# Mamba-2 layer with an FFN: the product between chunks taken out of the decay matrices, and four decay units a tile in place of six

## What is computed

```python
A_dt = (dt * A)                                    # per token and head, negative
A_cum = jnp.cumsum(A_dt, axis=-1)                  # within a chunk
L = jnp.exp(_segsum(A_dt))                         # exp(A_cum[l] - A_cum[s]) for s <= l
Y_diag = jnp.einsum('bzlhn,bzshn,bhzls,bzshp->bzlhp', Cc, Bc, L, xch)
decay_states = jnp.exp(A_cum[..., -1:] - A_cum)
states = jnp.einsum('bzlhn,bhzl,bzlhp->bzhpn', Bc, decay_states, xch)
...                                                # prev: the state ahead of a chunk
Y_off = jnp.einsum('bzlhn,bzhpn,bhzl->bzlhp', Cc, prev, jnp.exp(A_cum))
Y = (Y_diag + Y_off).reshape(b, s, H, P) + hs * D[None, None, :, None]
g = y * jax.nn.silu(gate)                          # then normed by group, times out_proj
```

## Time and profile before

| what | us |
|---|---|
| median of 3 runs | 1920.87 |
| lowest and highest | 1920.41, 1922.65 |
| the profiled execution | 1922.98 |
| its span in the profile | 1921.2 |

### The profile page before, as it was taken

One profiled execution on the slowest core, in us unless ns is written; L12 is line 12 of the kernel. 1 busy time (PEld: TensorE's weight loads), 2 busy tenths in 40 slices (PEclk: granted clock), 3 DMA queues, 4 the chain that ended last, 5 costly groups with the idle time before them and its releaser, 6 DMA issues.

```text
span 1921.2 us, 37314 instructions
## 1 busy us (share of the span) xinstructions
PE 1818.6 (95%) x11192; PEld 1482.3 (77%) x11192; DVE 1310.7 (68%) x2149; ACT 918.2 (48%) x1660; POOL 1014.9 (53%) x802
## 2 busy tenths in 40 slices
PE   4799999999999999999999999999999977989898
PEld 3577787778777877787778777877787756878887
DVE  6788738873887388638863886388638848777776
ACT  2566526653665366536653664366436632212221
POOL 6266636663666366636663666366536665333220
PEclk9899999999999999999999999999999988999999
DMA  2211101110111011101110111011101110111101
GB/s 90 60 52 49 37 12 51 51 33 12 51 51 33 12 51 51 33 12 51 51 33 12 51 51 33 12 51 51 33 12 52 40 41 22 45 44 34 42 11 45
DMA packets 43568, 74.83 MB, mean 39 GB/s; under 512 B 10321, under 2 KB 11473, under 8 KB 43537
## 3 DMA queue, kind: packets, MB, share of 16 engines
q1 hardware_dynamic: 43536, 74.43, 12.3%
HBM read 70.35 MB, written 4.06 MB: 39 GB/s over the span
## 4 chain that ended last, share of the span: by engine, by line
PE 87%; DVE 8%; issue 2%; ACT 1%; POOL 1%; DMA 0%; SPq 0%; DVEq 0%; POOLq 0%; ACTq 0%
PE proj L738 15%; PE proj L740 15%; PE proj L739 15%; PE y L870 6%; PE y L924 5%; PE y L926 5%; PE y L925 5%; PE y L860 3%; PE trb L837 3%; PE diff L846 3%; DVE gated L1229 2%; PE misc L846 1%; PE y L738 1%; PE y L739 1%; PE y L740 1%
## 5 line engine op out<-in xcount | busy, mean ns | idle before, releaser
L738 PE MATMUL proj<-xhi,w_hi 128*128 128x512 f32 x1088 | 464.8, 427 | 0.6 <-DVE v L1052 0.6
L740 PE MATMUL proj<-xhi,w_lo 128*128 128x512 f32 x1088 | 425.3, 391 | 0.0
L739 PE MATMUL proj<-xlo,w_hi 128*128 128x512 f32 x1088 | 424.7, 390 | 0.0
L391 POOL TENSOR_TENSOR w_lo<-w_raw,w_hi 128x512 fp32r<-128x512 f32 x144 | 183.6, 1294 | 223.6 <-ACT w_hi L516 223.6
L1052 DVE SCALAR_TENSOR_TENSOR v<-proj,par_sb,v 128x510 f32<-128x510 f32 (+2 forms) x384 | 281.8, 742 | 23.3 <-ACT v L538 19.9
L447 POOL TENSOR_TENSOR g_lo<-gated,g_hi 128x512 fp32r<-128x512 f32 x128 | 164.7, 1290 | 190.1 <-ACT g_hi L670 189.4
L738 PEld LDWEIGHTS proj<-xhi,w_hi 128*128 128x128 f32 x1088 | 204.5, 188 | 70.1 <-DVE v L1052 7.2
L740 PEld LDWEIGHTS proj<-xhi,w_lo 128*128 128x128 f32 x1088 | 204.2, 188 | 46.1
L739 PEld LDWEIGHTS proj<-xlo,w_hi 128*128 128x128 f32 x1088 | 204.8, 188 | 38.5
L1147 DVE TENSOR_TENSOR M<-diff,cb 128x512 f32<-128x512 f32 x256 | 170.3, 686 | 81.3 <-ACT diff L625 81.3
L924 PE MATMUL y<-wo_hi,g_hi 128*128 128x512 f32 x512 | 204.1, 399 | 5.5 <-POOL g_lo L447 5.1
(11 more groups left out here) (179 smaller groups left out, 3733.4 us busy)
## 6 DMA issues: line engine op xcount, KB each, us to landing
w_raw<-in_win SPq DMA_DIRECT2D x144, 256.0 KB, 2.7
wo_raw<-in_wout SPq DMA_DIRECT2D x64, 256.0 KB, 2.5
M<-in_w SPq DMA_DIRECT2D x14, 512.0 KB, 3.3
cb<-in_w SPq DMA_DIRECT2D x7, 512.0 KB, 3.3
row_l<-rows_l SPq DMA_DIRECT2D x192, 6.0 KB
resid<-in_x SPq DMA_DIRECT2D x8, 256.0 KB, 6.6
out<-resid SPq DMA_DIRECT2D x8, 256.0 KB, 2.0
rows_l<-gated SPq DMA_DIRECT2D x9, 128.0 KB, 2.5
```

The lines of the kernel that those rows point to most:

```text
L391: e.tensor_tensor(w_lo[:, slot, i, :], w_raw[:, i, :], w_hi[:, slot, i, :].bitcast(F32), ALU.subtract).then_inc(split.sem, 1)
L738: e.matmul(o, hi_l, hi_r, start=first, stop=False)
L739: e.matmul(o, hi_l, lo_r, start=False, stop=False)
L740: return e.matmul(o, lo_l, hi_r, start=False, stop=last)
```

## The change

The exponents of kind 1 (from chunk 0 to chunk 1) are gone, and with them two decay matrices a tile. Their part of y is made another way. The input of chunk 0 is weighted once with dt * exp(sum of what follows in the chunk) (`dt_rest`, made at the start; `xrest`, two VectorE operations of 256 columns a tile). One fp32 product per sequence, with C.B from chunk 0 to chunk 1 (`cb[:, 1]`) moving and xrest of both heads as the weights, goes to the bank misc (`y_past`). VectorE multiplies it with exp of the running sums of chunk 1 (`decayed`, loaded from DRAM and spread over the 64 partitions of a head; `scale_past`), and adds it to the second chunk of y, after the two sums (`late`). `y_own` holds the other 16 narrow products. The four decay units use two banks. Units 1 and 2 of the projection stand around exponents 2 and 3 now.

row_l is loaded from the same DRAM rows as row_r; the sign is in the rows of ones. Both are single, not doubled, so SyncE loads the next tile's rows when all four exponents of this tile are made. Behind scale_past it loads decayed, in two DMAs. GpSimd's gated waits for the last add in both halves. At the start, the reversed sums and the negated copies are gone.

```diff
-        row_r = sb("row_r", [P, 2, 2, TOK], BF16)
-        row_l = sb("row_l", [P, 2, 2, 3 * P], BF16)
+        row_r = sb("row_r", [P, 2, TOK], BF16)
+        row_l = sb("row_l", [P, 2, 2 * P], BF16)
+        dt_rest = sb("dt_rest", [P, B, H])
+        xrest = sb("xrest", [P, B, P])
+        decayed = sb("decayed", [P, HALF])
...
 # SyncE
             def step(g, j, par_, nxt, nxt2):
...
                 if nxt:
-                    sp.wait_ge(dready.sem, dready.at(g, j, 1))
-                    load_rows(TPG * g + j + 1, 1 - par_)
+                    sp.wait_ge(dready.sem, dready.at(g, j, UNITS))
+                    load_rows(TPG * g + j + 1)
                 if nxt2:
                     load_pair(9 * g + j + 3, split.at(g, j, 0))
+                if nxt:
+                    sp.wait_ge(scaled.sem, scaled.at(g, j, 1))
+                    load_decayed(TPG * g + j + 1)
...
 # GpSimd
                 for h in range(2):
-                    pool.wait_ge(ysum.sem, ysum.at(g, j, h + 1))
+                    pool.wait_ge(ysum.sem, ysum.at(g, j, 3))
...
 # ScalarE, step
                 decays(0)
...
                     tap3(0, w, ready.at(g, j, 1), silu.at(g, j, -1))
-                decay(2)
-                decay(3)
                 if nxt:
                     tap3(1, w, ready.at(g, j, 2), silu.at(g, j, 0))
                     act.wait_ge(gdone.sem, gdone.at(g, j, 0))
                     hs_tanh(hs[:, 1 - par_, :], 0, taken.at(g, j, 1))
+                decays(2)
                 if nxt2:
                     act.wait_ge(ready.sem, ready.at(g, j, 0))
                     upper_pair(par_, 9 * g + j + 3)
-                decays(4)
                 if nxt:
                     hs_tanh(hs[:, 1 - par_, :], 1, taken.at(g, j, 2))
...
 # TensorE, step
+                def y_past():
                     pe.wait_ge(xdts.sem, xdts.at(g, j, 2))
                     pe.wait_ge(ysum.sem, ysum.at(g, j, 0))
+                    for b in range(B):
+                        mm = e.matmul(misc[:, b * P:(b + 1) * P], xrest[:, b, :], cb[:, 1, b * P:(b + 1) * P],
+                                      start=True, stop=True)
+                    mm.then_inc(yready.sem, 1)
+
+                def y_own():
+                    pe.wait_ge(mdone.sem, mdone.at(g, j, UNITS))
...
                 turn(1)
+                if nxt:
+                    unit(1)
                 exponents(2)
                 exponents(3)
                 if nxt:
-                    unit(1)
-                y_first()
-                exponents(4)
-                exponents(5)
-                if nxt:
                     unit(2)
+                y_past()
+                if nxt:
                     unit(3)
-                y_second()
+                y_own()
...
 # VectorE, step
+                    early = trb[:, :].rearrange("p (b z a f) -> p z b a f", b=2, z=2, a=2)[:, 0, :, :, :]
+                    rest = dt_rest[:, 2 * h:2 * h + 2, bass.ds(2 * t, 2)].unsqueeze(3).broadcast_to([P, 2, 2, HD])
+                    e.tensor_tensor(xrest[:, 2 * h:2 * h + 2, :].rearrange("p b (a f) -> p b a f", a=2), early, rest,
+                                    ALU.mult)
...
+                def scale_past():
+                    dve.wait_ge(yready.sem, yready.at(g, j, 1))
+                    dve.wait_ge(s_grown, (TPG * 32) * g + 32 * j + 32)
+                    e.tensor_tensor(misc[:, :], misc[:, :], decayed[:, :], ALU.mult).then_inc(scaled.sem, 1)
...
                 if nxt:
-                    conv_rest(0, w, tap.at(g, j, 1), convs.at(g, j, 0),
-                              (lambda: weigh(2), lambda: weigh(3)))
+                    conv_rest(0, w, tap.at(g, j, 1), convs.at(g, j, 0))
                     conv_rest(1, w, tap.at(g, j, 2), convs.at(g, j, 2),
                               (lambda: hs_silu(hs[:, 1 - par_, :], 0, tanh.at(g, j, 1)),))
...
-                weigh(4)
-                weigh(5)
+                weigh(2)
+                weigh(3)
                 if nxt:
                     hs_silu(hs[:, 1 - par_, :], 1, tanh.at(g, j, 2))
                     gate_silu(gate[:, 1 - par_, :], 0, tanh.at(g, j, 3))
+                scale_past()
+                if nxt:
                     gate_silu(gate[:, 1 - par_, :], 1, tanh.at(g, j, 4))
...
+                dve.wait_ge(scaled.sem, scaled.at(g, j, 1))
+                dve.wait_ge(ysum.sem, ysum.at(g, j, 2))
+                late = y.rearrange("p (b z l) -> p z b l", b=B, z=2)[:, 1, :, :]
+                e.tensor_tensor(late, late, misc[:, :].rearrange("p (b l) -> p b l", b=B), ALU.add).then_inc(ysum.sem, 1)
```

More of the change, by code:

```diff
@@ L29 @@
 EPS = 1e-5
-UNITS = 6
-SLOT = [0, 1, 2, 3, 0, 1]
+UNITS = 4
 class Tally:
@@ L399, in _ @@
             split_pair(1, 2)
[L401 to L408, removed]
+            pool.wait_ge(s_part[0], 1)
+            e.tensor_tensor(rem, acum, r_part[:, 0, :], ALU.subtract).then_inc(s_rest, 1)
+            pool.wait_ge(s_rest, 1)
+            pool.wait_ge(s_part[1], 1)
+            e.tensor_tensor(r_part[:, 2, :], rem, r_part[:, 1, :], ALU.subtract).then_inc(s_part[2], 1)
             split_pair(1, 4)
@@ L807, in _ @@
             mm.then_inc(s_cum, 1)
-            for b in range(B):
-                mm = e.matmul(misc[:, b * P:(b + 1) * P], dta[:, 2 * b * P:(2 * b + 1) * P],
-                              after, start=True, stop=True)
-            mm.then_inc(s_cum, 1)
+            e.matmul(misc[:, :].rearrange("p (b h) -> p b h", b=B), after,
+                     dta.rearrange("p (b z h) -> p z b h", b=B, z=2)[:, 0, :, :], start=True, stop=True).then_inc(s_cum, 1)
             for n in range(CUM_AFTER + 1, 8):
@@ L850, in unit @@
+                    pe.wait_ge(mdone.sem, mdone.at(g, j, q - 1))
+                    at_l = row_r[:, head, :].rearrange("p (b z l) -> p z b l", b=B, z=2)[:, z, :, :]
+                    e.matmul(diff[q % 2][:, :].rearrange("p (b l) -> p b l", b=B),
+                             row_l[:, head, z * P:(z + 1) * P], at_l, start=True, stop=True).then_inc(dready.sem, 1)
                 def unit(n):
                     project(1 - par_, n // 2, n % 2, split.at(g, j, n // 2 - 1), taken.at(g, j, n - 1))
-                def y_first():
-                    pe.wait_ge(mdone.sem, mdone.at(g, j, 2))
+                def y_past():
@@ L858, in y_first @@
                     for b in range(B):
-                        for head in range(2):
-                            mm = e.matmul(ybank[b // 2][head * HD:(head + 1) * HD, (b % 2) * S:(b % 2) * S + P],
-                                          xdt[:, 2 * b, head * HD:(head + 1) * HD],
-                                          M[:, SLOT[head], b * P:(b + 1) * P], start=True, stop=True)
-                    mm.then_inc(yready.sem, 1)
-                def y_second():
-                    pe.wait_ge(mdone.sem, mdone.at(g, j, 6))
-                    for b in range(B):
-                        for part in range(2):
-                            for head in range(2):
-                                mm = e.matmul(
-                                    ybank[b // 2][head * HD:(head + 1) * HD, (b % 2) * S + P:(b % 2 + 1) * S],
-                                    xdt[:, 2 * b + part, head * HD:(head + 1) * HD],
-                                    M[:, SLOT[2 + 2 * part + head], b * P:(b + 1) * P],
-                                    start=(part == 0), stop=(part == 1))
+                        for z in range(2):
+                            for head in range(2):
+                                first = (b % 2) * S + z * P
+                                mm = e.matmul(ybank[b // 2][head * HD:(head + 1) * HD, first:first + P],
+                                              xdt[:, 2 * b + z, head * HD:(head + 1) * HD],
+                                              M[:, 2 * z + head, b * P:(b + 1) * P], start=True, stop=True)
```

110 lines of the change are left out of this document (48 added, 62 removed).

## The result

| | median us | runs | ratio to the kernel before, 95% interval |
|---|---|---|---|
| before, on the same chip | 1920.64 | 1920.28 to 1922.65 | |
| changed | 1937.92 | 1936.37 to 1942.58 | 1.009, 1.0078 to 1.0102 |

The change costs 17.3 us. The forecast was 1926 with 1916 to 1934 for its own case, and 1906 to 1944 in all: the sign is right and the wide range holds, the size is not right. The rival "Late weights decide" had 1943.

What follows compares the result with a forecast made beforehand. TensorE was taken to bound the kernel, 95% busy. Steps of 16.47 against 16.38 gave +5.7 us, the start -1.6, the last step +1: +5.1 on 1922.98, so 1928.1, a median of 1926, range 1906 to 1944.

Steps and rivals of the forecast that it cites:

- its own case: The forecast's likeliest case for the whole kernel: steps of 16.31 to 16.60, 1916 to 1934 us, chance 0.52.
- Late weights decide: Rival: late w_raw and hs_silu 1's wait for GpSimd delay VectorE; step 16.74, +23 us, 1943 us, chance 0.20.
- What TensorE does less: TensorE's step: two exponent products and y_first go, y_past comes; 0.63 us saved, 15.75 without any wait.
- The wait for the taps: TensorE ahead of unit 2 waits 0.62 us for VectorE's three taps of half 0, making the step 16.37.
- the 35 to 50 that were named: Sign: TensorE idle once a step ahead of unit 2, about 35 to 50 us in total.
- the rival with links of 0.67: Rival: taps follow each other like independent operations, weights cost nothing; steps 16.02 to 16.25, 1898 to 1912 us, chance 0.22.
- Up to here it costs nothing: Late weights on VectorE: free 2.0 into the next step, weighings end at 4.2, second transposes arrive at 4.43; no cost.
- the collision term: hs_silu 1 meets GpSimd's split, 0.3 us; with 0.15 for the last add's wait and branch, 0.1 a step.
- The lateness ahead of it: SyncE's w_raw loads behind the late row loads: w_raw there at 12.35 into the step, cast at 9.24 before.
- The range: Whole-kernel median of 1906 to 1944 us, leaving out the full gain and parts of two rivals.
- The start: Kernel start: two bc silus meet half as much GpSimd work, 3.23 becomes about 1.6, so -1.6 us.

Runs made afterwards that it cites:

- e4: Changed kernel with the w_raw loads ahead of the row loads and y_past ahead of unit 2: 1878.38 us, 0.9767 of before.
- e1: Changed kernel with the two w_raw loads ahead of the row loads in SyncE's queue: 1914.64 us, 0.9962 of before.
- e7: Changed kernel, GpSimd's split waiting for hs_silu 1 and its sums of squares for the next step's hs_silu 0: 1952.82 us, 1.0154 of before.
- e2: Changed kernel with GpSimd's split of w_raw waiting for hs_silu 1 of its step: 1920.7 us, 0.9991 of before.
- e8: Kernel before with row and w_raw loads issued late and ScalarE's w_raw casts behind the last two exponents: 1922.26 us, 1.0009 of before.
- e10: Changed kernel without the last add of each tile: 1917.31 us, 0.9978 of before.
- e9: Changed kernel with w_raw loads first, y_past ahead of unit 2 and GpSimd's start preparation done twice: 1888.57 us, 0.9828 of before.
- e6: Changed kernel with GpSimd's start preparation done a second time on scratch: 1939.8 us, 1.0086 of before.
- e3: Changed kernel with y_past ahead of unit 2 in TensorE's step, weights still late: 1924.45 us, 1.0015 of before.

## Why the prediction was half right

- **What TensorE does less** held. The step without waits was forecast at 15.75; e4, which has next to none, shows 15.85. y_past was a little cheaper than its 0.96: the next unit starts 0.81 behind it (368.68 to 369.49 in e4).
- **The wait for the taps** held to a tenth: unit 2 at 7.93 into a short step against 7.92, 34.5 us in 64 waits, just under the 35 to 50 that were named. The short steps are 16.40 against 16.37. e4 against e1 prices it: 16.45 - 15.88 = 0.57. The three taps of half 0 take 2.51 together (each 0.74 long, the last two starting 0.88 and 0.89 behind the ones ahead, where 0.91 and 0.78 were counted), so the rival with links of 0.67 is out. The Trainium skill, "VectorE: DVE Perf Modes", section "The DRAIN you can't avoid", says that a semaphore between chained Vector operations costs nothing extra. For these taps, which read what the one ahead wrote, the trace does not agree: 0.88 against 0.67 for two independent operations. The row of the taps:

```profile
396.43 2.51 DVE L1037 SCALAR_TENSOR_TENSOR v<-proj,par_sb,v 128x510 f32<-128x510 f32 x3
```

- **"Up to here it costs nothing"** is the step that failed. It had VectorE free 2.0 into the next step, 4.2 after the weighings, with 0.23 of slack to 4.43. e7, where nothing collides, has xrest at 2.75 and the second xrest at 4.88. The missing 0.75 are three small sizes: the tanh of gate 1 at 15.28, not 15.1; from its start to gate_silu 1 0.85 (340.84 to 341.69), not 0.63; and 1.00 from the last add to xrest where 0.60 was counted; the operations between came out 0.05 shorter. The 1.00 holds the loop's branch (0.31 idle for nothing that the profile shows), for which I had put 0.15 into the collision term. Slack that is a sum of ten rows was treated as exact. The lateness ahead of it was right: w_raw was forecast 12.35 into the step, and lands at 12.35 in the median.
- **The collision term** was mis-sized too. It had 0.3 for hs_silu 1, a cut at the first of GpSimd's two instructions. In 17 of 64 tiles it met the second and waited for nearly all of it, over 1.4 us and up to 1.84 in place of 0.69; in 45 it took under 0.75. Both terms together: forecast 0.10 a step, measured 16.77 - 16.45 = 0.32, of which 0.15 lateness (e7) and 0.17 collision (e2). That hs_silu 0 costs nothing was right.
- **The rival "Late weights decide"** had this mechanism, 16.74 a step and its point, a last add that ends later than about 2.2 into the next step. In e7 the add ends at 2.44 (343.71 + 0.69) and costs, and at 2.03 at the other border and does not; in the long step above it ends at 3.04. It should have had the larger chance. The runs add one condition: it needs the last add as well (e8, e10).
- **The range** was kept with some luck. The 56 steps cost 0.37 each where 0.09 was forecast, and the start gave back 6.9 us more than was forecast.
- **The start** was forecast at -1.6 and is -8.5. I read the two bc silus (3.23 to 1.79) and not the eight normalisations ahead of them, which lay beside GpSimd's selects on row_r. Halved rows mean halved selects, and by the end of the normalisations the changed kernel is 7.7 us ahead (28.08 against 35.75). Its VectorE:

```profile
14.58 0.99 DVE L1000 TENSOR_SCALAR gated<-resid,mv,rstd 128x512 f32<-128x512 f32 x2
...
19.00 2.32 DVE L1000 TENSOR_SCALAR gated<-resid,mv,rstd 128x512 f32<-128x512 f32 x1
21.84 1.57 DVE L1000 TENSOR_SCALAR gated<-resid,mv,rstd 128x512 f32<-128x512 f32 x1
...
26.02 0.66 DVE L1000 TENSOR_SCALAR gated<-resid,mv,rstd 128x512 f32<-128x512 f32 x1
```

The two ahead of the memsets and selects take 0.54 each, those beside the first memset and the selects 1.57 to 2.32, and the one at 26.02, which starts 0.38 before the end of a memset, 0.66. In the kernel before, beside a memset of 3.51 and selects of 3.72, four took 3.34 to 4.65. If the start is paid in full, as in e9, the change would have cost some 26 us without this gain; e6 showed no such price.

## What to carry to other kernels

When a transfer moves back in a queue, look first at what stands behind its consumer in that engine's order: the same late load cost 157 us, nothing or about 20 us, depending on what was queued behind the cast and how long the tail of VectorE was. The saving on the bounding engine was worth little here until the next two limits were gone together (e1 alone 0.9962 of before, e3 alone 1.0015, both 0.9767), so fill the new wait (y_past ahead of unit 2) and put the load back in one go. A slack worked out from many rows should be given an error before a term is set to nothing by it: this one was 0.23 us, and the sum behind it came out 0.7 too low.

## What the runs showed of the hardware

VectorE's operation on two SBUF tensors and a GpSimd operation on 512 columns exclude each other for their whole length, in either direction. In the changed kernel hs_silu waited (1.65 and 1.74 us against 0.69). All 74 of its 128 that took over 0.75 us end 0.55 behind the GpSimd instruction that they started in. In e4 it is the other way round too:

```profile
372.52 3.00 POOL L400 TENSOR_TENSOR w_lo<-w_raw,w_hi 128x512 fp32r<-128x512 f32 x2 [2.21 <-ACT w_hi L522]
```
```profile
373.53 0.84 DVE L1050 SCALAR_TENSOR_TENSOR hs<-hs,v 128x512 f32<-128x512 f32 x1
```

hs_silu loses 0.15 to the rest of the first half of the split, and the second half then waits for hs_silu: 3.00 for the two in place of 2.54. So a collision is priced by where in the other's instruction it falls, 0.15 or 1.05 us on VectorE. This agrees with the Trainium skill, "SBUF — State Buffer", section "SBUF: two separate sides", which calls the port pair shared by the two engines an exclusive lock that the first holds for its whole instruction. The normalisations, which read one tensor of 512 columns from SBUF, wait for GpSimd's memsets and selects as well. They did not wait for its operation on rstd, 128x4, which lay beside the two at 14.58.
